# Moving hosted node batches of a four-layer GNN kernel between passes: a quarter of the last node pair goes from the third score pass to the fourth dense slot pass

## The chip, the cores and the metric

One core of one Trainium2 chip runs the whole kernel as a single launch. The metric is the device time of one execution in microseconds (us). Time before: 5043.83 us, the median of three runs (5041.87, 5043.83 and 5056.84 us).

## The reference, cut to what matters

The network is a residual chain over 50,000 nodes and 25,000 edges (sorted by destination), all in float32 with 128 features:

```
x = LN(x + GAT3(x))        # three attention layers, 4 heads, softmax over incoming edges
x = LN(x + GCN2(x))        # two weighted graph convolutions, relu after each
x = LN(x + relu(GCN1(x)))  # one graph convolution
x = LN(x + SAGE2(x))       # relu([h, mean of neighbours] @ W + b), twice
```

Only nodes that are the destination of an edge need the sums over edges. For a node without incoming edges a layer is a dense product with its own row alone: for the SAGE stage `h1 = relu(h W1[0:128] + b1)`, `h2 = relu(h1 W2[0:128] + b2)`, `out = LN(h + h2)`. The intermediate `h1` is needed too, since edges gather it in the second SAGE layer.

## The kernel before, in words

**Tiles.** A batch is 512 rows (four groups `g` of 128), 256 KB. There are `nb` = 49 batches of edge slots and 2 x 49 = 98 batches of nodes. Each table in DRAM (`tables[0]` to `tables[7]`, `final`) has a slot part and a node part. Slot rows carry the destinations with edges, node rows carry every node as if it had none, and the last pass scatters the slot results over the node rows of the output.

**Stages.** The program runs stages one after the other, each in its own block with a barrier of all engines and a clearing of semaphores between two of them (`Semaphores.__exit__`). In order: structure, weights, a dense chain over the nodes, first slots, then three times `edge_scores`, `softmax` and `attend` (one attention layer each), then five passes of `convolve`: convolve(0) and (1) are the two weighted GCN layers, (2) the third GCN layer, (3) and (4) the two SAGE layers.

**Node work rides on edge stages.** `edge_scores` computes attention scores of the edge batches and beside them, on the otherwise free engine time, the dense pair "W1, relu, W2, relu, residual, layer norm" of node batches. For the third layer this pair is the SAGE pair (`third`), and its 98 node batches are spread over three places:

- `edge_scores(2, ..., 0, middle)` with `middle` = 25: 25 turns of one edge batch and two node batches (node batches 0 to 49), with the step orders `step_two`.
- `edge_scores(2, ..., middle, nb, True)` ("solo"): 24 turns of one edge batch and one node batch (the even ones, 50 to 96), with `step_solo`.
- convolve(0) "hosts" the odd ones from 49 to 97 (25 batches, 49 is computed twice), every second turn.

In the first part of a layer's pass with `start` = 0 the kernel also repairs the last rows of each tile (`patch`): POOL gathers `tails`, SP stores them back, and only then do the gathers and the loads of own rows begin.

**Turns and lags.** Every engine has its own hand-written order of steps. `skewed` calls `step(at)` once per turn n; `at(k)` is batch n - k, so a step with `at(3)` works three turns behind. `even(b)` restricts a hosted step to every second batch. All waits are semaphore waits in that in-order stream. Turns of different engines are tied only by these waits.

**convolve.** Per turn, POOL issues four indirect gathers of 128 rows (line 2540) and holds for b > 3 on `summed` of three batches ago. SP loads the batch's own rows (2488), stores the results (2500). DVE builds the selection matrix from a key (`build`, 2828 and 2832), adds the carry between tiles after PE's sum (`carry`, 1913 to 1920) and does the relu out of PSUM (`residual`, 2844). PE sums the edges (`sum_edges`, 2572), adds the own rows (`add_own`: GCN 2587 as a product with a diagonal into the same bank, SAGE 2582 as transposes into a bank of its own) and multiplies by the weights (`product`: 2596, in SAGE also 2599). ACT sets the bias (2698), and copies the sums out (`sums_out`: 2717, in SAGE first the transposed own rows, 2715); in GCN it also builds the diagonal (2702, 2706).

**Hosted chain of one node batch.** SP `load_nodes` (2470, holds on the read of the batch two hosted batches ago), PE `node_turn` (2608), ACT `node_turned` (2734), PE `node_hidden` (2613), ACT `node_relu` (2739), PE `node_middle` (2618), ACT `node_middle_out` (2745, 2747), PE `node_product` (2624), DVE `node_residual` (2880) and `node_moments` (2886, 2891), ACT `node_deviation` (2753), DVE `node_scale` (2897, 2899), ACT `node_normalise` (2759), and two stores on SP (2476, 2482). It has two `nx` and two `nz` buffers. In DVE's order `node_residual` stands behind `residual` of the same turn:

```
b = at(2)
if b:
    residual(b)
b = at(5)
if even(b):
    node_residual(b)
    node_moments(b)
```

Of the kernel before, what the change touches and what calls it, by code (L numbers as in the profile page):

```python
# [15 lines left out]
D = 128  # L16
# [131 lines left out]
def program(nc, io, n_nodes, n_edges):  # L148
# [5 lines left out]
    with ctx:  # L154
# [2250 lines left out]
        def convolve(n, mode, norm, t_in, t_out, t_res, weights, bias_io, nodes=None):  # L2405
# [4 lines left out]
            with ExitStack() as c, Semaphores(nc) as sem:  # L2410
# [35 lines left out]
                def even(b):  # L2446
                    return nodes and b and b.slot % 2 == 0
# [6 lines left out]
                with nc.Block() as block:  # L2454
                    @block.sync
                    def _(sp):
# [45 lines left out]
                        def step(at):  # L2502
                            b = at(0)
                            if b:
                                load_own(b)
                            b = at(1)
                            if b and norm:
                                load_residual(b)
                            b = at(3)
                            if even(b):  # L2510
                                load_nodes(b)
                            b = at(6 if norm else 4)
                            if b and not placing:
                                store(b)
                            b = at(6)
                            if even(b):
                                store_node_middle(b)
                            b = at(9)
                            if even(b):
                                store_nodes(b)  # L2520
                        skewed(sp, nb, 9 if nodes else 6 if norm else 4, step, 4)
# [34 lines left out]
                    def _(pe):  # L2556
# [71 lines left out]
                        def node_steps(at):  # L2628
                            b = at(4)
                            if even(b):  # L2630
                                node_middle(b)
                            b = at(5)
                            if even(b):
                                node_product(b)
                            b = at(3)
                            if even(b):
                                node_hidden(b)

                        def step_gcn_relu(at):
                            b = at(1)  # L2640
                            if b:
                                sum_edges(b)
                            node_steps(at)
                            b = at(2)
                            if b:
                                product(b)
                            if even(b):
# [38 lines left out]
                        if sage:  # L2686
                            skewed(pe, nb, 5 if nodes else 3 if norm else 2, step_sage_norm if norm else step_sage_relu, 4)
                        else:
                            skewed(pe, nb, 5 if nodes else 2, step_gcn_norm if norm else step_gcn_relu, 4)

                    @block.scalar
                    def _(act):
# [70 lines left out]
                        def node_steps(at):  # L2763
                            b = at(3)
                            if even(b):
                                node_relu(b)
                            b = at(4)
                            if even(b):
                                node_middle_out(b)
                            b = at(6)  # L2770
                            if even(b):
                                node_deviation(b)
                            b = at(7)
                            if even(b):
                                node_normalise(b)

                        def step_relu(at):
# [4 lines left out]
                            b = at(2 if sage else 1)  # L2782
# [3 lines left out]
                            b = at(2)  # L2786
# [31 lines left out]
                        else:  # L2818
                            skewed(act, nb, 7 if nodes else 2 if sage else 1, step_relu, 4)

                    @block.vector
                    def _(dve):
# [79 lines left out]
                        def step_relu(at):  # L2902
# [6 lines left out]
                            b = at(6)  # L2909
# [5 lines left out]
                            b = at(5)  # L2915
# [35 lines left out]
                        else:  # L2951
                            skewed(dve, nb, 6 if nodes else 2, step_relu, 4)
# [31 lines left out]
        convolve(0, "gcn0", False, t[3], t[4], None, (io["L1_gnn_W1"],), io["b_L1_gnn_b1"], third + (2 * (nb - middle) + 1,))  # L2984
        convolve(1, "gcn0", True, t[4], t[5], t[3], (io["L1_gnn_W2"],), io["b_L1_gnn_b2"])
        convolve(2, "gcn1", True, t[5], t[6], t[5], (io["L2_gnn_W"],), io["b_L2_gnn_b"])
        convolve(3, "sage", False, t[6], t[7], None, (io["L3_gnn_W1"][D:, :], io["L3_gnn_W1"][0:D, :]), io["b_L3_gnn_b1"])
# [63 lines left out]
```

How the kernel before makes its waits and increments, by code:

```python
def hold(eng, sem, value):  # L76
    if not isinstance(value, int) or value > 0:
        eng.wait_ge(sem, value)
# [12 lines left out]
    def step(self, ins):  # L92
        self.n += 1
        ins.then_inc(self.sem, 1)
        self.eng.wait_ge(self.sem, self.turn.count(self.per_turn, self.n) if self.turn else self.n)
# [122 lines left out]
        def segments(dve, ch, pe_sem, tr_sem, cnt, what, val):  # L218
# [3 lines left out]
            src, src2 = (keep, keep2) if what == "sum" else (pen, pen2)  # L222
            for d, out in ((0, seg_f), (1, seg_b)):
                rev = slice(None, None, -1) if d else slice(None)
                for h in range(4):
                    ins = nc.vector.tensor_tensor_scan(out[:, h, rev], src[:, d, rev], val[:, h, rev],
                                                       neutral, *ops)
                ch.step(ins)
                edge = 0 if d else ROW - 1
                nc.vector.tensor_copy(seg_t[:, :], out[:, :, edge]).then_inc(pe_sem, 1)
                cnt[0] += 1
                dve.wait_ge(tr_sem, cnt[0])
                ch.step(nc.vector.tensor_tensor_scan(seg_s[:, rev], src2[:, d, rev],
                                                     bank[0][0:4, 0:rq][:, rev], neutral, *ops))
                ch.step(nc.vector.memset(seg_c[:, :], neutral))
# [4 lines left out]
                ins.then_inc(pe_sem, 1)  # L240
                cnt[0] += 1
                dve.wait_ge(tr_sem, cnt[0])
                ch.step(nc.vector.tensor_copy(seg_t[:, :], bank[1][0:rq, 0:4]))
```

## Time and profile before

| what | us |
|---|---|
| median of three runs | 5043.83 |
| the profiled execution, its own time | 5052.05 |
| its span, first to last instruction | 5049.9 |
| third score pass, two-node part, 25 turns | 213.9 |
| third score pass, one-node part, 24 turns | 152.1 |
| convolve(0), which hosts, 49 turns | 272.9 |
| convolve(3), which hosts nothing, 49 turns | 257.5 |
| mean granted clock of TensorE (share of full speed) | 0.913 |

The stage times are distances between the barriers, read from the timeline. All durations further down come from the one profiled execution of 5052.05 us. That is 8.2 us over the median and within the three runs shown.

### The profile page before, as it was taken

What the parts mean: (1) busy time and instruction counts of PE and PEld (TensorE: products, weight loads), DVE (VectorE), ACT (ScalarE), POOL (GpSimd) and SP (SyncE); (2) the same over time, 40 slices, a digit from 0 to 9 for tenths busy, and PEclk for the clock granted to TensorE, in tenths of its full rate; (3) what the DMA queues carried; (4) which work ended last, traced back from release to release, by engine and by line L of the source; (5) the groups of instructions that cost most, each with busy time, mean ns of one, the idle gap of its engine ahead of it and who ended that gap; (6) DMA issues with size and microseconds to landing.
All of it is one profiled execution on the core that took longest, in us unless ns stands there. A gap on an engine that the chain in (4) does not pass through costs nothing. (4 is left out here: it accounts for less than half of the span.)

```text
span 5049.9 us, 108087 instructions
## 1 busy us (share of the span) xinstructions
PE 3969.3 (79%) x24378; PEld 2916.8 (58%) x24378; DVE 3727.1 (74%) x14651; ACT 3450.8 (68%) x11317; POOL 3018.4 (60%) x2914
## 2 busy tenths in 40 slices
PE   1999999797996898994998974997877666666554
PEld 1667667565774454873555752444766565665554
DVE  4899999545998787897886966997668787544433
ACT  0789999554886676894776863887878787333332
POOL 6888888255452122761224462887757676767777
PEclk9999999798998899997998997998998898997666
DMA  2566666487996576994777984775766565543332
GB/s 90 157 186 200 196 195 197 161 308 258 351 349 220 196 240 203 357 362 146 241 242 243 333 305 141 228 227 169 234 202 208 187 210 187 153 145 115 93 101 70
DMA packets 603571, 1061.32 MB, mean 210 GB/s; under 512 B 109737, under 2 KB 124603, under 8 KB 603373
## 3 DMA queue, kind: packets, MB, share of 16 engines
q1 hardware_dynamic: 521644, 920.61, 53.4%
q0 software_dynamic: 81728, 138.51, 10.6%
q8 instruction: 70, 1.15, 0.1%
q14 instruction: 129, 1.05, 0.1%
HBM read 608.75 MB, written 453.92 MB: 210 GB/s over the span
## 5 line engine op out<-in xcount | busy, mean ns | idle before, releaser
L2540 POOL DMA_INDIRECT got_c<-table,src_row x980 | 931.4, 950 | 387.7 <-issue 311.9
L1434 POOL DMA_INDIRECT src_got_s<-table,src_row x588 | 554.6, 943 | 445.9 <-issue 93.0
L2572 PE MATMUL bank<-pick_c,got_c 128*128 128x128 f32 x1960 | 333.3, 323 | 352.9 <-DMA got_c<-table,src_row 281.5
L2082 PE MATMUL bank<-w_all,dt_m 128*128 128x512 f32 x1176 | 569.2, 601 | 35.2 <-DMA dt_m<-delta_t 34.0
L2572 PEld LDWEIGHTS bank<-pick_c,got_c 128*128 128x128 f32 x1960 | 288.1, 226 | 396.5 <-issue 244.6
L2056 POOL TENSOR_TENSOR part_m<-part_m,half_sum_m 128x512 f32<-128x512 f32 x98 | 158.6, 1619 | 581.8 <-DVE half_sum_m L2289 581.8
L1607 ACT ACTIVATE z_s<-z_s,shift_s,dev_s 128x128 f32<-128x128 f32 x1080 | 444.0, 485 | 2.2 <-DVE shift_s L1745 1.3
L793 PEld LDWEIGHTS bank<-w_mean,ht 128*128 128x128 f32 x2352 | 312.1, 193 | 142.5 <-issue 142.5
L2596 PE MATMUL bank<-w_c,agg_c 128*128 128x128 f32 x1960 | 370.5, 315 | 4.0 <-ACT agg_c L2717 3.8
L2717 ACT COPY agg_c<-bank 128x512 f32<-128x512 f32 x245 | 142.8, 583 | 320.3 <-DVE bank L1920 274.5
L790 PE MATMUL bank<-bias,first_row 128*128 128x512 f32 x588 | 321.3, 628 | 38.0 <-ACT ht L853 13.8
L2082 PEld LDWEIGHTS bank<-w_all,dt_m 128*128 128x128 f32 x1176 | 210.2, 193 | 231.1 <-issue 133.7
L2596 PEld LDWEIGHTS bank<-w_c,agg_c 128*128 128x128 f32 x1960 | 325.1, 230 | 19.8 <-issue 11.5
L843 ACT ACTIVATE bank<-bank 128x128 f32<-128x128 f32 x1176 | 306.8, 261 | 42.0 <-PE bank L793 33.9
L2183 ACT ACTIVATE part_m<-bank,now_m 128x128 f32<-128x128 f32 x588 | 215.0, 366 | 157.7 <-PE bank L2082 141.2
L793 PE MATMUL bank<-w_mean,ht 128*128 128x128 f32 x2352 | 313.2, 277 | 0.0
L2728 ACT ACTIVATE z_c<-z_c,shift_c,dev_c 128x128 f32<-128x128 f32 x588 | 242.2, 482 | 89.0 <-DVE shift_c L2868 89.0
L2832 DVE TENSOR_SCALAR pick_c<-iota,now_c 128x128 f32<-128x128 f32 x980 | 282.3, 365 | 11.8 <-DVE now_c L2828 0.5
L754 POOL TENSOR_TENSOR rows<-rows 128x512 f32<-128x512 f32 x196 | 260.5, 1329 | 42.9 <-DVE rows L925 40.7
L2061 POOL DMA_INDIRECT x_m<-in_x_dram,dst_node x196 | 222.0, 1133 | 98.5 <-issue 52.0
L1913 DVE COPY tails_c<-tails_c 128x1 f32<-128x1 f32 x245 | 37.5, 153 | 328.4 <-PE bank L2572 322.5
L2289 DVE SCALAR_TENSOR_TENSOR part_m<-bank,now_m,part_m 128x128 f32<-128x128 f32 x588 | 203.6, 346 | 69.5 <-ACT half_sum_m L2184 68.2
(352 smaller groups left out, 11912.6 us busy)
## 6 DMA issues: line engine op xcount, KB each, us to landing
table<-rows SPq DMA_DIRECT2D x294, 256.0 KB
x_s<-table SPq DMA_DIRECT2D x270, 256.0 KB
x_c<-table SPq DMA_DIRECT2D x245, 256.0 KB
table<-z_s SPq DMA_DIRECT2D x196, 256.0 KB
table<-z_c SPq DMA_DIRECT2D x196, 256.0 KB
table<-mid_s SPq DMA_DIRECT2D x172, 256.0 KB
own_rows_s<-table SPq DMA_DIRECT2D x147, 256.0 KB
pick_t_s<-picks_t SPq DMA_DIRECT2D x147, 256.0 KB
```

The source lines that it names most:

```text
L754: nc.gpsimd.tensor_tensor(flat(rows[l + 1][r]), flat(rows[l + 1][r]), flat(rows[l][r]), ALU.add).then_inc(summed[l], 1)
L790: nc.tensor.matmul(b_y[l][:, :], first_row[:, :], bias[:, l, :, :].rearrange("p g d -> p (g d)"), start=True, stop=False, skip_group_check ...
L793: ins = nc.tensor.matmul(b_y[l][:, g * D:(g + 1) * D], ht[l][b.half][:, g, :], w_mean[:, l, :], start=False, stop=True, skip_group_check=True)
L843: ins = nc.scalar.activation(bank[7][:, g * D:(g + 1) * D], b_y[l][:, g * D:(g + 1) * D], ACT.Square, accum_out=square[l][r][:, g:g + 1])
L1434: nc.gpsimd.indirect_dma_start(out=src_got[r][:, g, :], out_offset=None, in_=tables[l].rows, in_offset=bass.IndirectOffsetOnAxis(ap=src_ro ...
L1607: ins = nc.scalar.activation(v[:, g, :], v[:, g, :], ACT.Identity, bias=shift[side(b, h)][:, g:g + 1], scale=dev[side(b, h)][:, g:g + 1])
L2082: nc.tensor.matmul(b_h[k % n_h][:, :], dt[b.slot][:, k, :], w_all[:, l, :, :].rearrange("p h d -> p (h d)"), start=True, stop=True).then_i ...
L2540: nc.gpsimd.indirect_dma_start(out=got[r][:, g, :], out_offset=None, in_=t_in.rows, in_offset=bass.IndirectOffsetOnAxis(ap=src_row[:, t:t ...
L2572: ins = nc.tensor.matmul(b_sum[r][:, k * P:(k + 1) * P], got[b.slot][:, k, :], pick[r][:, k, :], start=k == 0, stop=sage, skip_group_check ...
L2596: ins = nc.tensor.matmul(b_y[r][:, k * D:(k + 1) * D], agg[r][:, k, :], ws[0][:, :], start=False, stop=True, skip_group_check=True)
L2728: ins = nc.scalar.activation(z[b.slot][:, g, :], z[b.slot][:, g, :], ACT.Identity, bias=shift[r][:, g:g + 1], scale=dev[r][:, g:g + 1])
L2832: ins = nc.vector.tensor_scalar(pick[r][:, k, :], iota[:, :], now[r][:, k, KEY:KEY + 1], now[r][:, k, COEF + m:COEF + m + 1], ALU.is_equal ...
```

## The change

It does four things. The third score pass becomes one part of 49 turns in its one-node form, which covers the even node batches 0 to 96. convolve(0) hosts the same odd batches 49 to 97 as before. convolve(3), the first SAGE pass, hosts the odd batches 1 to 49. In every hosted pass all steps of the hosted chain come two turns sooner (the load three), and the pass has two turns less at its end. In a SAGE pass that hosts, ACT copies the sums out one turn sooner (`at(1)` in place of `at(2)`).

```diff
@@ SP in convolve
-                            b = at(3)
+                            b = at(0)
                             if even(b):
                                 load_nodes(b)
                             b = at(6 if norm else 4)
                             if b and not placing:
                                 store(b)
-                            b = at(6)
+                            b = at(4)
                             if even(b):
                                 store_node_middle(b)
-                            b = at(9)
+                            b = at(7)
                             if even(b):
                                 store_nodes(b)
-                        skewed(sp, nb, 9 if nodes else 6 if norm else 4, step, 4)
+                        skewed(sp, nb, 7 if nodes else 6 if norm else 4, step, 4)
@@ PE in convolve: node_middle at(4) to at(2), node_product at(5) to at(3), node_hidden at(3) to at(1)
                             b = at(2)
                             if b:
                                 product(b)
+                            b = at(0)
                             if even(b):
                                 node_turn(b)
...
-                            skewed(pe, nb, 5 if nodes else 3 if norm else 2, step_sage_norm if norm else step_sage_relu, 4)
+                            skewed(pe, nb, 3 if nodes or norm else 2, step_sage_norm if norm else step_sage_relu, 4)
                         else:
-                            skewed(pe, nb, 5 if nodes else 2, step_gcn_norm if norm else step_gcn_relu, 4)
+                            skewed(pe, nb, 3 if nodes else 2, step_gcn_norm if norm else step_gcn_relu, 4)
@@ ACT in convolve: node_relu at(3) to at(1), node_middle_out at(4) to at(2), node_deviation at(6) to at(4), node_normalise at(7) to at(5)
                             node_steps(at)
-                            b = at(2 if sage else 1)
+                            b = at(2 if sage and not nodes else 1)
                             if b:
                                 set_bias(b)
                                 sums_out(b)
-                            b = at(2)
+                            b = at(0)
                             if even(b):
                                 node_turned(b)
...
-                            skewed(act, nb, 7 if nodes else 2 if sage else 1, step_relu, 4)
+                            skewed(act, nb, 5 if nodes else 2 if sage else 1, step_relu, 4)
@@ DVE in convolve: node_scale at(6) to at(4), node_residual and node_moments at(5) to at(3)
-                            skewed(dve, nb, 6 if nodes else 2, step_relu, 4)
+                            skewed(dve, nb, 4 if nodes else 2, step_relu, 4)
@@ the program
-        middle = (nb + 1) // 2
+        spare = nb // 2 * 2 + 1
         third = (t[6], t[7], t[8], (io["L3_gnn_W1"][0:D, :], io["c_L3_gnn_b1"]), (io["L3_gnn_W2"][0:D, :], io["b_L3_gnn_b2"]))
-        edge_scores(2, third[3], third[4], *third[0:3], 0, middle)
-        edge_scores(2, third[3], third[4], *third[0:3], middle, nb, True)
+        edge_scores(2, third[3], third[4], *third[0:3], 0, nb, True)
         softmax(2)
         attend(2)
-        convolve(0, ..., third + (2 * (nb - middle) + 1,))
+        convolve(0, ..., third + (spare,))
         ...
-        convolve(3, "sage", False, t[6], t[7], None, ..., io["b_L3_gnn_b1"])
+        convolve(3, "sage", False, t[6], t[7], None, ..., io["b_L3_gnn_b1"], third + (1,))
```

## Rows read from the trace of the kernel before

**Rows 1.** The page, part 1: busy us, share of the span, instructions.

```profile
PE 3969.3 (79%) x24378; PEld 2916.8 (58%) x24378; DVE 3727.1 (74%) x14651; ACT 3450.8 (68%) x11317; POOL 3018.4 (60%) x2914
```

**Rows 2.** Windows, four stages: stretch, length, busy PE PEld DVE ACT POOL, clock, DMA, GB/s.

```profile
2704.50:2918.40 213.90, 192.04 (x1404) 150.14 (x1404) 177.29 (x675) 163.88 (x401) 96.39 (x102) 0.94 0.90 311
2918.40:3070.50 152.10, 119.45 (x916) 87.97 (x916) 95.22 (x336) 90.56 (x217) 90.61 (x96) 0.94 0.86 294
3487.30:3760.20 272.90, 221.11 (x1632) 191.41 (x1632) 177.13 (x766) 217.81 (x569) 185.31 (x196) 0.96 0.69 216
4284.40:4541.90 257.50, 173.34 (x1376) 160.91 (x1376) 125.42 (x491) 82.99 (x148) 186.15 (x196) 0.96 0.51 152
```

**Rows 3.** Windows of the steady middle of the one-node and the two-node part.

```profile
2950.00:3040.00 90.00, 78.45 (x635) 58.83 (x634) 65.56 (x231) 62.34 (x150) 66.54 (x71) 1.00 0.99 340
2750.00:2870.00 120.00, 118.32 (x902) 93.02 (x901) 113.83 (x434) 105.25 (x259) 61.33 (x66) 1.00 1.01 353
```

**Rows 4.** Line 1712, once per turn: two-node part, then one-node part.

```profile
L1712 DVE TENSOR_TENSOR delta_s<-src_got_s,bank x25: 653/686/690, 2725.9 to 2905.5; 128x512 f32<-128x512 f32 x25
...
L1712 DVE TENSOR_TENSOR delta_s<-src_got_s,bank x24: 672/673/686, 2931.7 to 3057.2; 128x512 f32<-128x512 f32 x24
```

**Rows 5.** The longest wait of PE in the steady one-node part: total, times, longest.

```profile
PEld bank L1501 <- DVE delta_s L1712: 18.8, 12, 1.6
```

**Rows 6.** The gathers of line 2540 in convolve(0), then in convolve(3).

```profile
L2540 POOL DMA_INDIRECT got_c<-table,src_row x196: 940/944/1048, 3488.3 to 3732.2; - x196
...
L2540 POOL DMA_INDIRECT got_c<-table,src_row x196: 940/944/1061, 4285.8 to 4530.5; - x196
```

**Rows 7.** Line 2880, once per hosted batch, in convolve(0).

```profile
L2880 DVE SCALAR_TENSOR_TENSOR nz_c<-bank,nx_c x25: 678/680/693, 3519.1 to 3752.7; 128x512 f32<-128x512 f32 x25
```

**Rows 8.** Timeline of convolve(0), its last full pair of turns and its end.

```profile
3731.16 0.68 DVE L2880 SCALAR_TENSOR_TENSOR nz_c<-bank,nx_c 128x512 f32<-128x512 f32 x1
3731.93 0.34 SPq L2470 DMA_DIRECT2D nx_c<-table  x1
...
3734.94 0.63 PE L2608 MATMUL bank<-ident,nx_c 128*128 128x128 f32 x4 [0.84 <-ACT nmid_c L2745]
3735.40 1.06 PE L2587 MATMUL bank<-own_c,x_c 128*128 128x128 f32 x8
...
3736.50 1.16 PE L2572 MATMUL bank<-pick_c,got_c 128*128 128x128 f32 x8
3737.50 1.06 PE L2624 MATMUL bank<-nw_c,nht_c 128*128 128x128 f32 x8
...
3738.39 1.02 PE L2613 MATMUL bank<-nxt_c,nw_c 128*128 128x512 f32 x2
3739.25 1.05 PE L2596 MATMUL bank<-w_c,agg_c 128*128 128x128 f32 x8
...
3740.34 0.69 DVE L2844 TENSOR_SCALAR z_c<-bank 128x512 f32<-128x512 f32 x1 [1.95 <-PE bank L2596]
3740.95 0.68 DVE L2880 SCALAR_TENSOR_TENSOR nz_c<-bank,nx_c 128x512 f32<-128x512 f32 x1
...
3742.72 1.16 PE L2596 MATMUL bank<-w_c,agg_c 128*128 128x128 f32 x8 [1.09 <-ACT agg_c L2717]
...
3745.08 0.66 PE L2608 MATMUL bank<-ident,nx_c 128*128 128x128 f32 x4 [1.20 <-DMA nx_c<-table]
...
3755.55 1.65 ACT L2759 ACTIVATE nz_c<-nz_c,nshift_c,ndev_c 128x128 f32<-128x128 f32 x4 [0.44 <-DVE nshift_c L2899]
```

**Rows 9.** Timeline of one turn of convolve(3).

```profile
4401.89 0.58 ACT L2715 COPY own_c<-bank 128x512 f32<-128x512 f32 x1
...
4402.75 1.13 PE L2572 MATMUL bank<-pick_c,got_c 128*128 128x128 f32 x8 [1.82 <-DVE pick_c L2832]
4403.72 0.39 PE L2596 MATMUL bank<-w_c,agg_c 128*128 128x128 f32 x2
...
4405.50 0.60 PE L2582 MATMUL bank<-ident,x_c 128*128 128x128 f32 x4
```

More of the change, by code:

```diff
@@ L2628, in node_steps @@
                         def node_steps(at):
-                            b = at(4)
+                            b = at(2)
                             if even(b):
                                 node_middle(b)
-                            b = at(5)
+                            b = at(3)
                             if even(b):
                                 node_product(b)
-                            b = at(3)
+                            b = at(1)
                             if even(b):
@@ L2763, in node_steps @@
                         def node_steps(at):
-                            b = at(3)
+                            b = at(1)
                             if even(b):
                                 node_relu(b)
+                            b = at(2)
+                            if even(b):
+                                node_middle_out(b)
                             b = at(4)
                             if even(b):
-                                node_middle_out(b)
-                            b = at(6)
-                            if even(b):
                                 node_deviation(b)
-                            b = at(7)
+                            b = at(5)
                             if even(b):
@@ L2785, in step_relu @@
                                 sums_out(b)
-                            b = at(2)
+                            b = at(0)
                             if even(b):
@@ L2908, in step_relu @@
                                 carry_over(b)
-                            b = at(6)
+                            b = at(4)
                             if even(b):
@@ L2914, in step_relu @@
                                 residual(b)
-                            b = at(5)
+                            b = at(3)
                             if even(b):
@@ L2977, in program @@
         attend(1)
-        middle = (nb + 1) // 2
+        spare = nb // 2 * 2 + 1
         third = (t[6], t[7], t[8], (io["L3_gnn_W1"][0:D, :], io["c_L3_gnn_b1"]), (io["L3_gnn_W2"][0:D, :], io["b_L3_gnn_b2"]))
-        edge_scores(2, third[3], third[4], *third[0:3], 0, middle)
-        edge_scores(2, third[3], third[4], *third[0:3], middle, nb, True)
+        edge_scores(2, third[3], third[4], *third[0:3], 0, nb, True)
         softmax(2)
         attend(2)
-        convolve(0, "gcn0", False, t[3], t[4], None, (io["L1_gnn_W1"],), io["b_L1_gnn_b1"], third + (2 * (nb - middle) + 1,))
+        convolve(0, "gcn0", False, t[3], t[4], None, (io["L1_gnn_W1"],), io["b_L1_gnn_b1"], third + (spare,))
         convolve(1, "gcn0", True, t[4], t[5], t[3], (io["L1_gnn_W2"],), io["b_L1_gnn_b2"])
         convolve(2, "gcn1", True, t[5], t[6], t[5], (io["L2_gnn_W"],), io["b_L2_gnn_b"])
-        convolve(3, "sage", False, t[6], t[7], None, (io["L3_gnn_W1"][D:, :], io["L3_gnn_W1"][0:D, :]), io["b_L3_gnn_b1"])
+        convolve(3, "sage", False, t[6], t[7], None, (io["L3_gnn_W1"][D:, :], io["L3_gnn_W1"][0:D, :]), io["b_L3_gnn_b1"], third + (1,))
         convolve(4, "sage", True, t[7], t[8], t[6], (io["L3_gnn_W2"][D:, :], io["L3_gnn_W2"][0:D, :]), io["b_L3_gnn_b2"])
```

## The prediction

> **What bounds the kernel now.** The page comes first: PE is busy 79% of the span, DVE 74%, POOL 60% [rows 1]. No engine is full, so the share says little and each stage has to be read for itself. The stages are serial, with a barrier between two of them. So the time of a change is the sum of what it does to the length of each stage that it touches, and the windows give those: 213.9 us for the two-node part of the third score pass, 152.1 for its one-node part, 272.9 for convolve(0), 257.5 for convolve(3) [rows 2].
>
> In the two-node part PE is the bound: busy 118.3 of 120 us in the steady middle [rows 3]. A turn takes (2905.5 - 2725.9) / 24 = 7.48 us [rows 4]. In the one-node part PE is busy 78.5 of 90 us and POOL 66.5 of 90 [rows 3]; PE waits for DVE's difference and DVE for PE, a chain over engines inside a turn [rows 5]. Its turn takes (3057.2 - 2931.7) / 23 = 5.46 us [rows 4].
>
> The convolve passes are bound by something else. POOL issues 196 gathers in (3732.2 - 3488.3) us in convolve(0) and in (4530.5 - 4285.8) us in convolve(3) [rows 6]. Over 195 intervals that is 1.251 and 1.255 us each, 5.00 and 5.02 us per turn of four. Both passes run at POOL's pace although one hosts node work and the other doesn't. What the hosting costs before is the tail: from the last gather's issue to the barrier convolve(0) takes 3760.2 - 3732.2 = 28.0 us, convolve(3) 4541.9 - 4530.5 = 11.4 us [rows 2, 6].
>
> The reading in a sentence: a node batch costs 7.48 - 5.46 = 2.0 us as second node batch in the score pass, and nearly nothing in a pass that waits for POOL anyway.
>
> **Part 1, the score pass in one part.** Before: 213.9 + 152.1 = 366.0 us [rows 2]. After: 49 one-node turns. The head comes from the two-node part, since that one has the repair of tile tails in front: 2725.9 - 2704.5 = 21.4 us to the first use of line 1712 (the one-node part, without the repair, needs 2931.7 - 2918.4 = 13.3). Then 48 turns of 5.46 = 262.1 us. Then the end of the one-node part, 3070.5 - 3057.2 = 13.3 us [rows 2, 4]. The sum is 296.8, so this part gives **-69.2 us**. A barrier, a head of 13.3 and an end are saved once, and 25 turns shrink by 2.0 us each. Bounds of the turn: not under POOL's 5.0 us [rows 6], which would give 22 us more; not over the two-node turn of 7.48, which does strictly more. I take 5.46, since it is the same code. The SP queue gets per turn the same DMAs that it has now in the one-node part.
>
> **Part 2, hosted steps two turns sooner in convolve(0).** In the body every hosted step keeps its place relative to the others and the parity of its turn, so nothing changes there: POOL still sets 5.0 us. Only SP's load comes three turns sooner in its order and not two. It holds on the read of the `nx` buffer by line 2880, and now that hold stands in front of the stores and the two next loads of own rows. Those are needed two turns later and more, and a load lands in about 3 us (3731.93 to 3734.94, [rows 8]), so I cost it at nothing; if that cover were gone PE would wait for own rows. At the end the last node batch was turned at 3745.08, two turns after 3734.94, and the barrier came at 3760.2 [rows 2, 8]. Now the last batch takes the place that the one before it had, 10.1 us sooner. But its steps then stand between the edge steps of the last real turns instead of in empty ones. Its chain, step by step from rows 8: hidden 3738.4; last edge product after the copy at 3742.7; node product right behind at 3743.8; then what the old last batch needed from its own residual to the barrier. That was 3760.2 - 3752.7 = 7.5 us [rows 2, 7], and the residual comes at about 3744.9, or at 3746 if it has to wait for the store of its `nz` buffer. Barrier at 3752.4 to 3753.5: **-7 us** (bounds 0 and -10).
>
> **Part 3, hosting in convolve(3).** Added per pair of turns: three DMAs of 256 KB on SP, PE's 4 + 4 transposes, hidden and product, five ACT operations and the normalise, DVE's residual, moments and scale. Three questions.
>
> First, the tail. It follows the chain of part 2: last sum, node product, hidden, product, last product, node product, 7.5 us. I expect about 20.5 us where convolve(3) had 11.4: **+9 us**, and 1 us for the second weight product in it.
>
> Second, the ring that closes over two turns: residual of a node batch, load into its buffer, `node_turn`, own rows, sum, node product, hidden, product, `residual`, `node_residual`. In convolve(0) it is, from rows 8: 0.77 + 3.01 + 0.46 + 1.10 + 1.00 + 0.89 + 0.86 + 1.09 + 0.61 = 9.79 us, just under POOL's 10.0 for two turns. The mean over the 22 periods from 3519.1 to 3740.95 is 10.08 [rows 7, 8]. In SAGE the own rows are transposes, about 0.46 like `node_turn`, in place of 1.10: -0.64. The product is twice as many matmuls, 4405.50 - 4403.72 = 1.78 in place of about 0.89 [rows 9]: +0.89. So the ring is 10.04 at its fastest and 10.08 + 0.25 = 10.33 by the mean. It then is as long as POOL's ten or a bit longer, and has nothing left to catch up with. 24 pairs times 0.04 to 0.33 is 1 to 8 us. I take **+7 us**, nearer to the mean, since landings vary.
>
> Third, ACT's copies, which move a turn sooner. In rows 8 a sum's copy ends 4.3 us after hidden starts (3738.39 to the product at 3742.72), and SAGE adds the copy of own rows, 0.58 us by the same kind of copy (convolve(3) does one a turn). PE wants it after hidden 0.86, product 1.78, transposes 0.46, sum 0.97 and middle 0.46, that is 4.5 us [rows 8, 9]. So PE waits about 0.4 us once per pair. But `node_turn` then waits for its load in any case: 0.86 + 1.98 + 0.61 + 0.77 + 3.01 = 7.2 us after hidden, against 4.9 + 1.78 = 6.7. The wait is covered by the ring; without that cover it would cost 24 x 0.4 = 10 us.
>
> What POOL does is not altered. In convolve(0) DVE is busy 177.1 us with the hosted steps, in convolve(3) 125.4, and POOL's gathers come every 1.251 and 1.255 us [rows 2, 6]: hosted DVE work does not slow them. The Trainium skill (SBUF — State Buffer, section SBUF: two separate sides) speaks against this change here: it says that GpSimd and certain DVE operations take turns on a shared port, so that descriptors for gathers can't be written meanwhile. The trace disagrees for these operations, as the 1.251 us shows.
>
> **The sum.** -69 - 7 + 10 + 7 = -59 us. Against the profiled execution's own 5052.05 that is 4993. This execution lies 8.2 us over the median of 5043.83, so I forecast **4985 us**. TensorE's granted clock stays as it is in these windows: 1.00 in the steady parts, 0.94 to 0.96 with heads and tails [rows 2, 3].
>
> **The rivals.**
>
> *POOL's pace holds in convolve(3).* The ring comes out at its fast value of 10.04. For it: convolve(0) holds 5.00 with a ring of 9.79. Against it: nothing is left to catch up a late landing. The +7 becomes about 0: 4977 us.
>
> *The copies bind every turn.* If PE's product waited for ACT each turn as in the last full turn of convolve(0), 1.09 us [rows 8], a pair of turns would cost PE's own work plus 2.2. That work is 2 x (0.46 + 0.97 + 1.78) + 0.46 + 0.86 + 0.46 + 0.89 = 9.1 us, so a pair takes 11.3, and 24 x 1.3 = 31 in place of 7: 5009 us. For it: the margin above is only 0.5 us. Against it: ACT has 83 of 257 us busy there now [rows 2].
>
> *POOL stands still while DVE does hosted work.* Hosted DVE work per turn is about (177.1 - 125.4) / 49 = 1.1 us net of what GCN and SAGE share [rows 2]. If that held POOL, 49 x 1.1 = 52 us would come on top of convolve(3), in place of the 7: 5030 us. The gather intervals speak against it. This is the rule of the Trainium skill named above.
>
> *The long one-node pass is slower than its half: slower than before.* The 16 DMA engines show a share of 0.99 in it already, at 340 GB/s [rows 3]. A pass of 24 turns can live on lead and buffers where one of 49 can't, and the gathers would be late. The price is at most the two-node turn: 48 x (7.48 - 5.46) = 97 us more, 5082 us. It decides from the point where a turn takes 5.46 + 59 / 48 = 6.7 us. Against it: the two-node part moved 353 GB/s steadily [rows 3], and the 23 turns show no growth that would lead there.
>
> *The earlier steps don't shorten the tail.* The last node batch waits for an edge step and the barrier stays: 7 to 10 us lost, 4994 us.
>
> **How the numbers follow.** Forecast 0.60; POOL's pace holds 0.18; tail not shorter 0.05; copies bind 0.11; POOL held by DVE 0.02; long pass slower 0.02; the rest for smaller mishaps near the forecast. The range goes from 4966 (POOL's pace, tails at their good bounds, a median that falls as low as the runs before) to 5008 (just to the copies case). About 0.3% (15 us, the spread of the runs before) is what a measurement of this kernel can tell from no change, so faster means under 5029: 0.95. Same 0.03, slower 0.02.
>
> **What the profile after would show.** Line 1712 49 times in one stage of about 297 us, 5.4 to 5.6 apart; a stage over 310 makes part 1 wrong. Line 2540 in convolve(0) as before, and its barrier about 20 to 21 us after the last gather. In convolve(3) line 2608 100 times with a wait for `nx_c`, line 2880 10.0 to 10.4 apart, gathers 5.0 apart, the stage at 271 to 276 us. A wait of PE's 2596 for ACT's 2717 over 0.5 us in most turns would make the third point wrong; gathers over 1.3 us apart without a hold would bring the port back in.

## The result, and the profile after

The changed kernel takes **4979.83 us** (median of 4 runs, 4972.77 to 4991.71) against 5046.00 for the kernel before on the same chip (4 runs, 5041.87 to 5056.84). The ratio is 0.9868 with a 95% interval of 0.9843 to 0.9893: 66 us or 1.3% faster. The forecast was 4985.

The profiled execution of the changed kernel took 4980.41 us, its span is 4978.6, and the page's part 1 answers to [rows 1] almost unchanged:

```profile
PE 3945.6 (79%) x24376; PEld 2889.4 (58%) x24376; DVE 3694.1 (74%) x14601; ACT 3468.5 (70%) x11366; POOL 3017.6 (61%) x2914
```

The same work is done by the same engines (99 node batches in all before and after, 25 of them moved from the score pass into convolve(3)), so the shares tell nothing of the gain. The stages do. Windows of the changed kernel, from barrier to barrier, in the columns of [rows 2]: the third score pass, convolve(0), convolve(3).

```profile
2696.90:2994.70 297.80, 239.58 (x1866) 177.48 (x1866) 194.13 (x686) 184.39 (x442) 187.00 (x198) 0.96 0.90 306
3412.20:3678.20 266.00, 218.68 (x1632) 191.45 (x1632) 176.65 (x766) 217.56 (x569) 185.70 (x196) 0.97 0.70 222
4201.60:4470.10 268.50, 237.32 (x1828) 210.44 (x1828) 173.76 (x766) 175.55 (x373) 186.12 (x196) 0.97 0.69 220
```

| stage | before | after | measured | forecast |
|---|---|---|---|---|
| third score pass | 213.9 + 152.1 = 366.0 | 297.8 | -68.2 | -69.2 |
| convolve(0) | 272.9 | 266.0 | -6.9 | -7 |
| convolve(3) | 257.5 | 268.5 | +11.0 | +17 |
| sum | 896.4 | 832.3 | -64.1 | -59 |

The profiled executions differ by 5052.05 - 4980.41 = 71.6 us. The 7.5 us beyond the sum lie mostly in stages that the change doesn't touch: the barrier in front of the third score pass comes at 2696.9 instead of 2704.5. Such stages move by several us from one execution to the next, so 64 us is the change's part, and the medians' 66.2 agree.

The two-node part is gone, and the one-node turn is what it was. Line 1712 of the changed kernel, once per turn, beside [rows 4]:

```profile
L1712 DVE TENSOR_TENSOR delta_s<-src_got_s,bank x49: 669/673/686, 2718.6 to 2982.6; 128x512 f32<-128x512 f32 x49
```

(2982.6 - 2718.6) / 48 = 5.50 us per turn over the whole length. The gathers of line 2540 in convolve(0) and convolve(3) of the changed kernel, beside [rows 6], and the residual of the hosted batches in both (line 2882, the line 2880 of [rows 7]):

```profile
L2540 POOL DMA_INDIRECT got_c<-table,src_row x196: 938/944/1056, 3413.3 to 3657.5; - x196
...
L2540 POOL DMA_INDIRECT got_c<-table,src_row x196: 940/944/1054, 4202.7 to 4447.3; - x196
...
L2882 DVE SCALAR_TENSOR_TENSOR nz_c<-bank,nx_c x25: 678/681/693, 3436.0 to 3670.6; 128x512 f32<-128x512 f32 x25
...
L2882 DVE SCALAR_TENSOR_TENSOR nz_c<-bank,nx_c x25: 678/681/692, 4227.2 to 4462.7; 128x512 f32<-128x512 f32 x25
```

The gathers of convolve(3) take 244.6 us from first to last; without hosting they took 4530.5 - 4285.8 = 244.7. That is 1.254 us each against 1.255: the body of the pass didn't get longer at all. All of the +11 is tail: 4470.1 - 4447.3 = 22.8 us from the last gather to the barrier, where it was 11.4. In convolve(0) the tail went from 28.0 to 3678.2 - 3657.5 = 20.7 us.

Timeline of the changed kernel, one pair of turns in convolve(3), the ring that the prediction feared (start, duration, engine, line; in brackets the engine's idle time before it and what ended it):

```profile
4327.34 0.68 DVE L2882 SCALAR_TENSOR_TENSOR nz_c<-bank,nx_c 128x512 f32<-128x512 f32 x1
...
4328.27 0.35 SPq L2470 DMA_DIRECT2D nx_c<-table  x1
...
4328.70 0.30 PEld L2596 LDWEIGHTS bank<-w_c,agg_c 128*128 128x128 f32 x2 [0.27 <-ACT agg_c L2719]
...
4331.01 0.66 PE L2608 MATMUL bank<-ident,nx_c 128*128 128x128 f32 x4 [0.26 <-DMA nx_c<-table]
...
4331.50 0.60 PE L2582 MATMUL bank<-ident,x_c 128*128 128x128 f32 x4
...
4331.94 1.06 PE L2572 MATMUL bank<-pick_c,got_c 128*128 128x128 f32 x8
...
4332.83 1.06 PE L2624 MATMUL bank<-nw_c,nht_c 128*128 128x128 f32 x8
...
4333.73 1.02 PE L2613 MATMUL bank<-nxt_c,nw_c 128*128 128x512 f32 x2
...
4334.59 0.39 PE L2596 MATMUL bank<-w_c,agg_c 128*128 128x128 f32 x2
...
4336.57 0.69 DVE L2846 TENSOR_SCALAR z_c<-bank 128x512 f32<-128x512 f32 x1 [1.81 <-PE bank L2599]
...
4337.18 0.68 DVE L2882 SCALAR_TENSOR_TENSOR nz_c<-bank,nx_c 128x512 f32<-128x512 f32 x1
```

From residual to residual: 0.93 to the load's issue, 2.74 to its landing, then 0.49 + 0.44 + 0.89 + 0.90 + 0.86 + 1.98 + 0.61, in sum 9.84 us, under POOL's 10.03 for two turns (eight gathers at 244.6 / 195 us). PE waits 0.26 us for the load, and its weight load 0.27 us for ACT's copy of the sum.

### The profile page after: what moved, and what is told of

It reads as the page before. It is cut to its first block and busy times, and to the rows that moved or that the text cites. A ratio compares the mean times of both kernels' runs of the same rounds, so it can differ in the third digit from the quotient of the medians.

```text
span 4978.6 us, 108273 instructions
## 1 busy us (share of the span) xinstructions
PE 3945.6 (79%) x24376; PEld 2889.4 (58%) x24376; DVE 3694.1 (74%) x14601; ACT 3468.5 (70%) x11366; POOL 3017.6 (61%) x2914
## 5 line engine op out<-in xcount | busy, mean ns | idle before, releaser
L1607 ACT ACTIVATE z_s<-z_s,shift_s,dev_s 128x128 f32<-128x128 f32 x980 | 403.0, 485 | 2.0 <-DVE shift_s L1745 0.9
```

What stands on the lines that cost most here:

```text
L1607: ins = nc.scalar.activation(v[:, g, :], v[:, g, :], ACT.Identity, bias=shift[side(b, h)][:, g:g + 1], scale=dev[side(b, h)][:, g:g + 1])
```

## The experiments

They ran on three chips, four kernels on each. One, called A here, is like that of the result: the kernel before takes 5044.89 us there (median of 7). On B and C it takes 5604.75 and 5661.18 (one run each): the stages with gathers are longer there, for a cause that stays open (see the last section). So stages are compared within a chip. Three kernels ran on B and again on C, and one on B and again on A. All of these are single runs but `last_batch_once`, which has four. The stage lengths are barrier to barrier, from windows.

**What does hosting cost and save in all?** Nothing is hosted; all node batches sit in a two-node score pass in one part:

```
-        edge_scores(2, third[3], third[4], *third[0:3], 0, nb, True)
+        edge_scores(2, third[3], third[4], *third[0:3], 0, nb)
-        convolve(0, ..., third + (spare,))
+        convolve(0, ...)
-        convolve(3, ..., third + (1,))
+        convolve(3, ...)
```

> All 98 node batches in a two-node third score pass of 49 turns, nothing hosted in convolve(0) and convolve(3); the whole computation is done. My theory (a node batch costs 2.0 us as second one in the score pass and only a tail where it is hosted): score pass 213.9 + 24 x 7.48 = 393 us against 297.8 of the changed kernel; convolve(0) falls from 266.0 to about 258 and convolve(3) from 268.5 to 257.5. In sum some 76 us slower than the changed kernel, about 5056. Rival (hosted work stretches the POOL-paced passes by its engine time): convolve(0) and (3) would fall by more than their tails, to under 250 us, and their gathers would come closer than 1.25 us apart.

On B: 5567.87 us, stages 404.8, 305.5 and 303.8. The expected numbers were those of the result's chip. The same kernel on a chip like it:

> The kernel of all_in_pair_pass once more, for a second chip. As before: score pass 393 us, convolve(0) about 258, convolve(3) 257.5, in sum some 76 us slower than the changed kernel, where POOL's gathers come 1.25 us apart.

On A: 5054.82 us. Windows of the three stages:

```profile
2696.10:3088.80 392.70, 367.22 (x2748) 286.35 (x2748) 347.60 (x1323) 321.30 (x785) 186.93 (x198) 0.98 0.95 330
3506.00:3762.90 256.90, 183.94 (x1180) 169.53 (x1180) 127.82 (x491) 121.68 (x344) 185.41 (x196) 0.85 0.51 152
4286.60:4544.90 258.30, 173.23 (x1376) 160.69 (x1376) 124.75 (x491) 82.94 (x148) 186.25 (x196) 0.96 0.50 151
```

The stages came as expected (393, 258 and 257.5 us). They are three points of one ledger. Nothing hosted: 392.7 + 256.9 + 258.3 = 907.9. One pass hosts (before): 896.4. Two passes host (after): 832.3. A pass that hosts a quarter pays 266.0 - 256.9 = 9.1 us in convolve(0) and 268.5 - 258.3 = 10.2 in convolve(3); with the late steps of before it paid 16.0. The second quarter takes 68.2 us off the score pass, the first only 26.7, because it also split the pass in two. The next kernel measures that:

**How much of the 68 us is the barrier?** The one-node pass in two parts, hosting as in the changed kernel (names of tiles and semaphores of the second part apart):

```
-        edge_scores(2, third[3], third[4], *third[0:3], 0, nb, True)
+        edge_scores(2, third[3], third[4], *third[0:3], 0, middle, True)
+        edge_scores(2, third[3], third[4], *third[0:3], middle, nb, True)
```

> The changed kernel with its one-node score pass cut at 25 edge batches into two stages with a barrier between. My theory (the cut costs a second head of 13.3 and a second end of 13.3 us, less one turn of 5.46 that the two ends share): both parts together 297.8 + 21 = 319 us. So of the 68 us that the third score pass gained about 21 are the barrier and about 47 the cheaper turns. Rival (all of the gain is cheaper turns, the barrier costs its few instructions): under 300 us.

> The kernel of one_node_in_two_parts once more. My theory: both parts together 297.8 + 21 = 319 us, the barrier with its second head and end; the rest as in the changed kernel. Rival (the barrier costs its few instructions): under 300 us.

On B, 5583.21 us; the windows of the two parts:

```profile
2813.00:3017.20 204.20, 133.14 (x954) 97.68 (x954) 100.43 (x350) 93.81 (x226) 96.66 (x102) 0.88 0.71 229
3017.20:3205.80 188.60, 130.84 (x916) 96.57 (x916) 96.03 (x336) 90.25 (x217) 90.75 (x96) 0.89 0.73 237
```

Sum 392.8, where a kernel with one part takes 371.8 on the same chip (the next but one): +21.0. On C, 5667.88 us: 206.6 + 188.4 = 395.0 against 370.1: +24.9. So a second part costs 21 to 25 us on these two chips; it wasn't run on a chip like A, where the expectation of 21 rests on the rows of before. If it costs the same there, what is left of the 68, some 43 to 47 us, is the cheaper turns of 25 batches. That evens out the ledger above: 26.7 + 21 to 25 for the first quarter, 68.2 less as much for the second, 43 to 52 us each. The prediction's own split was a head of 13.3, an end, and 25 turns at 2.0 us.

**Are the sooner steps worth 7 us alone?** The placement of before, two passes and all, with the sooner steps:

```
+        middle = (nb + 1) // 2
-        edge_scores(2, third[3], third[4], *third[0:3], 0, nb, True)
+        edge_scores(2, third[3], third[4], *third[0:3], 0, middle)
+        edge_scores(2, third[3], third[4], *third[0:3], middle, nb, True)
-        convolve(3, ..., third + (1,))
+        convolve(3, ...)
```

> The kernel before with the earlier hosted steps alone; distribution of the node batches as before. My theory: only the end of convolve(0) changes, 272.9 to 266 us, every other stage as before, so 7 us faster than the kernel before. Rival (the last node batch waits for the edge steps anyway): convolve(0) stays within 1 us of 272.9. Rival (the load, now in front of the stores in SP's order, delays them): convolve(0)'s body grows and line 2880 comes more than 10.2 us apart.

> The kernel of steps_sooner_only once more. My theory: convolve(0) 266 us in place of 272.9, two-node part 213.9 and one-node part 152.1 as before, so 7 us faster than the kernel before, some 5038. Rival (the last node batch waits anyway): convolve(0) within 1 us of 272.9.

On B 5607.01 us against 5604.75 of the kernel before, on C 5648.38 against 5661.18. One run each, differences of both signs, and no profile of the kernel before on these chips whose convolve(0) could be set beside theirs (328.6 and 332.0). This is inconclusive: no run shows the sooner steps alone on a chip like A. The -7 rests on convolve(0) before and after, 272.9 to 266.0, where the step order is all that differs; the after side came again as 266.0 in `last_batch_once`, the before side is one execution.

**What is the copy a turn sooner worth?** ACT copies the sums at the old place in the hosting pass too:

```
-                            b = at(2 if sage and not nodes else 1)
+                            b = at(2 if sage else 1)
```

> The changed kernel, but ACT copies the sums of the hosting SAGE pass at(2) again. My theory: PE's product of a turn then waits for a copy that ACT makes in the same turn behind its hosted steps: about 4 us in the turns with relu and normalise (0.69 + 1.65 + 0.58 + 0.58 + 0.58 after hidden), about 3 us in the others, so a pair of turns takes about 16 us in place of 10 and convolve(3) about 268 + 24 x 6 = 412 us. Rival (buffers and slack cover it, the move is worth nothing): convolve(3) stays within 5 us of 268.5.

> The kernel of sums_at_two once more. There a pair of turns took 19.8 us, (5136.9 - 4662.2) / 24, against my 16, with PE waiting 3.0 to 3.8 us per turn for ACT's copy and its product of 16 matmuls taking 3.4 us in place of 1.8 behind the wait. Theory A (that chip was slow in all): 16 us a pair here, convolve(3) about 412 us. Theory B (the waits let TensorE's granted clock fall, so the wait costs twice): 19 to 20 us a pair here too, convolve(3) about 505 to 515, and a granted clock well under 1 in its windows.

On B 5778.98 us, convolve(3) 527.7 where the sooner copy takes 331.8 there; on C 5812.70 us, 528.1 against 334.7. That is far more than expected. The windows on B of the whole stage and of four us inside a turn, then rows of the product in two turns that follow each other:

```profile
4616.80:5144.50 527.70, 338.05 (x1828) 308.38 (x1828) 173.64 (x766) 175.57 (x373) 185.52 (x196) 0.75 0.36 112
4816.00:4820.00 4.00, 3.90 (x18) 3.90 (x19) 0.08 (x1) 0.04 (x1) 0.00 (x0) 0.50 0.06 16
```

```profile
4816.10 0.80 PE L2596 MATMUL bank<-w_c,agg_c 128*128 128x128 f32 x2 [3.78 <-ACT agg_c L2719]
...
4819.67 1.06 PE L2582 MATMUL bank<-ident,x_c 128*128 128x128 f32 x4
...
4825.64 0.80 PE L2596 MATMUL bank<-w_c,agg_c 128*128 128x128 f32 x2 [2.87 <-issue]
```

The copy stands behind ACT's hosted steps in the very turn that needs it. PE idles 3.78 us for it in one turn and 2.87 in the next, and then works at a granted clock of 0.50, which is 1.2 of 2.4 GHz: from the start of the product of 16 matmuls to the next step it takes 4819.67 - 4816.10 = 3.57 us instead of 1.78 [rows 9]. The mean clock of the stage is 0.75. The changed kernel has 0.93 over its convolve(3) on C, so it is not the chip. The wait costs twice: itself, and slower matmuls after it. The Trainium skill (TensorE: Matmul & The Clock Gate, section The HAM clock gate) says that PE gets its full or half its clock by how busy it has been; the 0.50 behind an idle 3.78 us agrees. A pair of turns takes (5136.9 - 4662.2) / 24 = 19.8 us in the mean with the short last one, by line 2882:

```profile
L2882 DVE SCALAR_TENSOR_TENSOR nz_c<-bank,nx_c x25: 678/680/692, 4662.2 to 5136.9; 128x512 f32<-128x512 f32 x25
```

It wasn't run on a chip like A, so the price there is open. But POOL waits in this pass for PE's sums, 228.5 us on B and 228.7 on C, so the pace of the gathers doesn't set its length, and an estimate for A is the same 528 us, some 260 over the 268.5 of the changed kernel. What it shows is that the sooner copy is not a detail but a condition for hosting in this pass at all.

**Is POOL or the ring the bound in convolve(3)?** Two kernels bend the ring, one each way. In the first, the load of a node batch waits for the end of DVE's moments and not only of its residual:

```
-                            hold(sp, nz_read, b.ring(1, -2))
+                            hold(sp, nz_stat, b.ring(1, -2))
```

> The changed kernel; SP's load of a hosted batch waits for the moments of the batch before the last and not only for its residual, which lengthens the ring of two turns by 1.4 us (2882 to the end of 2893 is 2.1 us, the residual alone 0.7). My theory (a ring of 9.8 to 10.0 us stands right below POOL's 10.0): a pair of turns takes 11.2 to 11.4 us in both hosting passes, so convolve(0) and convolve(3) grow by about 24 x 1.25 = 30 us each. Rival (POOL alone sets the pace and the ring has room): both within 3 us of 266.0 and 268.5, or of what the same chip shows for the changed kernel.

On A: 5065.68 us. Windows of convolve(0) and convolve(3), and line 2882 in convolve(3):

```profile
3412.20:3721.00 308.80, 231.66 (x1632) 206.43 (x1632) 176.91 (x766) 217.39 (x569) 185.62 (x196) 0.91 0.60 191
4245.50:4555.70 310.20, 245.65 (x1828) 220.92 (x1828) 177.20 (x766) 176.03 (x373) 185.28 (x196) 0.94 0.60 191
```

```profile
L2882 DVE SCALAR_TENSOR_TENSOR nz_c<-bank,nx_c x25: 679/680/692, 4269.8 to 4548.1; 128x512 f32<-128x512 f32 x25
```

Both stages grow by 42.8 and 41.7 us, where 30 were expected. The mean of the 24 periods in convolve(3) is (4548.1 - 4269.8) / 24 = 11.60 us, but they aren't alike. The last, in the tail, is 4.5 us as in the changed kernel. Of the other 23, 16 lie between 11.1 and 11.5 us (mean 11.32) and 7 between 13.1 and 13.7 (mean 13.25). Windows of a long pair and of one us in it; then rows of the long pair and of a plain one:

```profile
4294.27:4307.47 13.20, 10.98 (x77) 10.07 (x76) 7.19 (x33) 7.06 (x16) 10.14 (x11) 0.87 0.61 196
4301.00:4302.00 1.00, 1.00 (x7) 1.00 (x6) 0.00 (x0) 0.03 (x1) 0.69 (x2) 0.50 1.00 381
```

```profile
4299.66 0.75 PE L2608 MATMUL bank<-ident,nx_c 128*128 128x128 f32 x4 [1.99 <-DMA nx_c<-table]
...
4301.06 1.92 PE L2572 MATMUL bank<-pick_c,got_c 128*128 128x128 f32 x8
...
4407.71 0.68 DVE L2882 SCALAR_TENSOR_TENSOR nz_c<-bank,nx_c 128x512 f32<-128x512 f32 x1
...
4410.10 0.35 SPq L2470 DMA_DIRECT2D nx_c<-table  x1
```

In the plain pair the issue comes 2.39 us after the residual's start instead of 0.93, +1.46. Taken from 11.32 that leaves 9.86 for the ring as it was, beside the 9.84 read directly. The ring of the changed kernel thus stands some 0.2 us under POOL's 10.03. In the long pairs TensorE pays twice, as in `sums_at_two`: it waited 1.88 to 2.53 us for the load, its granted clock fell to 0.50 behind that (0.87 or 0.88 over each of these pairs), and the sum of 8 matmuls took 1.92 us instead of 1.06. In the plain pairs it waited 1.55 to 1.87 us and kept 1.00. So of the growth some 23 x (11.32 - 10.03) = 30 us are the longer ring, as expected, and 7 x (13.25 - 11.32) = 14 the clock.

In the second, DVE does the residual of the hosted batch ahead of that of the edges, which lets the load start sooner:

```
+                            b = at(3)
+                            if even(b):
+                                node_residual(b)
                             b = at(2)
                             if b:
                                 residual(b)
                             b = at(3)
                             if even(b):
-                                node_residual(b)
                                 node_moments(b)
```

> The changed kernel; in DVE's order node_residual stands in front of residual of the same turn, so the ring no longer contains PE's hidden product, the edge product and that residual: some 3 us shorter. My theory (POOL's 10.0 us already held in the changed kernel): the waits of line 2608 for nx_c vanish, 26 us in convolve(3) and 42 in convolve(0), and the stages get at most 2 us shorter. Rival (the ring costs the body something): convolve(3) gets 5 us or more shorter.

On A: 4983.23 us, convolve(0) 267.1, convolve(3) 268.6, within 1.1 and 0.1 us of the changed kernel. What PE waits for ahead of line 2608 in convolve(3), first in the changed kernel, then in this one (us, times):

```profile
L2608 PE MATMUL bank<-ident,nx_c x100: 272/273/418, 4213.7 to 4452.4; 128*128 128x128 f32 x100
...
  DMA nx_c<-table: 25.7, 45
```

```profile
L2608 PE MATMUL bank<-ident,nx_c x100: 272/273/421, 4216.4 to 4454.4; 128*128 128x128 f32 x100
...
  issue: 1.1, 2
```

All 25.7 us of waiting for the load vanish and the stage doesn't move by more than 0.1 us. (In convolve(0) the wait for the load falls from 41.6 to 1.0 us too, but PE stands 44.2 us for other things ahead of the same line.) The ring isn't the bound; POOL is, and PE's wait for the load was time that it had anyway. POOL's own waits for PE's sum in convolve(3) say the same (us in total, times, longest), first in the changed kernel, then in `load_waits_longer`:

```profile
POOL got_c L2540 <- PE bank L2572: 7.3, 24, 0.3
...
POOL got_c L2540 <- PE bank L2572: 37.5, 23, 3.4
```

The sum that POOL holds on is that of four batches before, whose buffer it fills again. In the changed kernel it never stands longer for it than 0.3 us, and that is what it idles ahead of any gather.

**What is the extra batch worth?** With an odd number of batches, batch 49 is computed by convolve(0) and once more by convolve(3). Here convolve(3) leaves it out:

```
-                    n_own = (nb + 1) // 2
+                    n_own = (nb + 1) // 2 - (offset == 1)
...
-                    return nodes and b and b.slot % 2 == 0
+                    return nodes and b and b.slot % 2 == 0 and not (
+                        offset == 1 and isinstance(b.i, int) and b.batch() == nb - 1)
```

> The changed kernel, but convolve(3) leaves out its 25th hosted batch (node batch 49), which convolve(0) computes as well; nothing of the result is missing. My theory: convolve(3)'s tail is the chain of the last node batch; now the batch before it ends it, so the barrier comes 4 to 8 us sooner, 268.5 to about 263 us, and no other stage changes. Rival (the last edge batch holds the end): under 1 us.

On A: 4978.68 us (median of 4 runs, 4972.18 to 4986.30) against 5044.89, ratio 0.987, interval 0.9851 to 0.9888. Window of convolve(3):

```profile
4204.70:4466.80 262.10, 234.01 (x1810) 208.09 (x1810) 170.79 (x755) 171.43 (x364) 185.76 (x196) 0.97 0.70 223
```

262.1 against 268.5: 6.4 us of the 11 were the tail of a batch that need not be there. The other stages are unchanged. In the whole time 6 us are less than the runs resolve (its ratio and that of the changed kernel overlap), so this is the best version by its stage, not shown by its total.

**Does the gain hold on a slower chip?** The changed kernel itself on C:

> The changed kernel itself, as the reference for the others of this call on the same chip. Where POOL's gathers come 1.25 us apart: score pass 297.8, convolve(0) 266.0, convolve(3) 268.5 us, all within 1 us.

5626.20 us against 5661.18 of the kernel before, one run each: -35 us, 0.6%. Line 1712 in the score pass, and the windows of the score pass and convolve(3):

```profile
L1712 DVE TENSOR_TENSOR delta_s<-src_got_s,bank x49: 670/674/689, 2858.6 to 3195.6; 128x512 f32<-128x512 f32 x49
```

```profile
2837.60:3207.70 370.10, 258.17 (x1866) 191.58 (x1866) 197.47 (x686) 183.58 (x442) 187.40 (x198) 0.91 0.77 246
4637.50:4972.20 334.70, 251.08 (x1828) 221.71 (x1828) 176.63 (x766) 175.95 (x373) 186.39 (x196) 0.93 0.58 177
```

A one-node turn takes (3195.6 - 2858.6) / 48 = 7.02 us there. The two-node part of `steps_sooner_only_2` on the same chip:

```profile
L1712 DVE TENSOR_TENSOR delta_s<-src_got_s,bank x25: 652/686/689, 2868.5 to 3061.7; 128x512 f32<-128x512 f32 x25
```

That is (3061.7 - 2868.5) / 24 = 8.05 us, so a second node batch costs 1.0 us there, not 2.0. In the score pass the change gains 227.9 + 189.2 - 370.1 = 47.0 us, of which 24.9 are the barrier. Hosting in convolve(3) costs 334.7 - 307.4 = 27.3 us, not 11. So the cheaper turns (22 us) don't pay for the hosting, and what remains is about the barrier. Whether the kernel that hosts nothing is the better one there stays open. By stages on B it takes 404.8 + 305.5 + 303.8 = 1014.1 us, and the changed placement 371.8 + 328.1 + 331.8 = 1031.7, put together from two kernels. But by whole times it takes 5567.87 us, and `one_node_in_two_parts` less its 21.0 for the second part 5562. The changed kernel itself didn't run on B.

## Why the prediction was right, step by step

**Part 1, the score pass: right.** Forecast 21.4 + 262.1 + 13.3 = 296.8; measured 2718.6 - 2696.9 = 21.7, then 264.0, then 2994.7 - 2982.6 = 12.1, in sum 297.8. The turn is 5.50 for 5.46 over twice the length: lead and buffers of the short pass were not what kept it fast. The rival "the long one-node pass is slower" fell on this chip. On C the turn is 7.02 us, over the 6.7 from which it was to decide, but not by that rival's mechanism: the DMA engines show a share of 0.77 there instead of 0.90, and the one-node part of 24 turns in `steps_sooner_only_2` is as slow (189.2 us for 152.1). What bounds the one-node turn of 5.50 us, the chain between PE and DVE or the DMA engines with their share of 0.99 [rows 3], no run separates.

**Part 2, convolve(0): right.** Forecast -7 with a barrier 20 to 21 us after the last gather; measured -6.9 and 20.7. That the load three turns sooner costs nothing held. The wait ahead of PE's last product for ACT's copy is still 1.09 us, as in [rows 8], and the chain from the last residual to the barrier is 3678.2 - 3670.6 = 7.6 for 7.5.

**Part 3, tail: right, 1.4 us short.** Forecast +10 with the second weight product; measured +11.4. Timeline of the tail in convolve(3) of the changed kernel:

```profile
4459.52 0.49 PE L2596 MATMUL bank<-w_c,agg_c 128*128 128x128 f32 x2 [1.56 <-ACT agg_c L2719]
...
4462.65 0.69 DVE L2882 SCALAR_TENSOR_TENSOR nz_c<-bank,nx_c 128x512 f32<-128x512 f32 x1 [0.35 <-PE bank L2624]
```

From the last residual to the barrier 4470.1 - 4462.65 = 7.45, the forecast's 7.5. The 1.56 us for ACT's copy are 0.5 more than in convolve(0), about one copy of own rows (0.58 us), which ACT does in SAGE only. The rest of the 1.4 us wasn't traced.

**Part 3, ring: the mis-sized term, +7 that measured 0.** The terms of the fast ring were near: 10.04 forecast, 9.84 in the pair shown and 9.86 by `load_waits_longer`. The landing took 2.74 instead of 3.01 us, the issue 0.93 instead of 0.77. What failed is the step "10.08 + 0.25 = 10.33 by the mean". The 10.08 was the period of a pass that POOL paces at 10.00; the ring inside it was shorter and waited. Adding the ring's growth to a period that another chain sets counts slack as cost. The right form is the larger of the two, POOL's 10.03 or the ring, and the body's 244.6 us says that it is POOL's. So the rival "POOL's pace holds in convolve(3)" came out (4977 forecast, 4980 measured). `node_residual_first` shows that shortening the ring gains nothing, `load_waits_longer` that it has some 0.2 us of room to grow. The forecast of the whole came near in spite of this because the term is small beside the 66 us.

**Part 3, copies: right.** Forecast: a wait of about 0.4 us once per pair, covered. In the pair shown it is 0.27 us on the weight load and none on the matmul, and the body is no longer than without hosting. "The copies bind every turn" fell; `sums_at_two` shows what that rival looks like when it is real.

**The rival that POOL stands still: refuted.** With hosted DVE work the gathers come every 1.254 us, without it every 1.255. The Trainium skill (SBUF — State Buffer, section SBUF: two separate sides) says that GpSimd and certain DVE operations lock each other out of a shared port, and names those in a two-port mode or with two inputs in SBUF. The hosted residual has one of its two inputs in PSUM, and the hosted operations as a whole show nothing of a lock here. So this isn't evidence against the rule, and the prediction read it too widely where it set it against this change.

**Range and sum.** The sum was -59 and the stages gave -64.1; the difference is in the main the 7 us of the ring less the small misses of the score pass (1.0) and the tail (1.4). 4979.83 lies inside 4966 to 5008.

## What to carry to other kernels

Look for passes paced by something that isn't computation (here gathers at 1.25 us each): dense work put into them cost its tail, 9 to 11 us per pass, while the same work in a pass bound by TensorE cost 2 us a batch and a barrier with head and end another 21 to 25. Measure it on each chip: on C the hosting cost 27 us. Where a ring of dependences runs beside a pace that another engine sets, take the larger of the two, never their sum, and measure how near they are before leaning on it: here 1.46 us more in the ring cost 42 us per pass. When a copy serves a later matmul, put it ahead of hosted steps on its engine; waits of TensorE of 1.88 to 3.78 us were paid twice in the runs here, the second time as a lower clock.

## What was not expected of the hardware

**Stages with gathers differ from chip to chip.** On B and C every convolve pass measured takes 300 us or more, and the one-node score pass 370. POOL in convolve(3) of the changed kernel on C, and the same gathers there in the kernel without hosting in it (`steps_sooner_only_2`):

```profile
4703.59 1.04 POOL L2540 DMA_INDIRECT got_c<-table,src_row  x1 [1.41 <-DMA table<-nmid_c]
```

```profile
L2540 POOL DMA_INDIRECT got_c<-table,src_row x196: 938/944/990, 4686.3 to 4976.0; - x196
```

The gather itself takes the same 0.94 us, but in the changed kernel the first of a turn's four is mostly preceded by an idle 1.3 to 1.5 us instead of 0.30; without hosting such idle times are fewer, and many of them are 2.3 us. There the mean spacing is (4976.0 - 4686.3) / 195 = 1.49 us against 1.255 on the result's chip. The trace names a store of `nmid_c` as what ended the wait, but `steps_sooner_only_2` issues no such store in this pass, so the releaser is not to be trusted. Nor is it POOL alone. In the score pass of the changed kernel on C four engines stand at the same time:

```profile
3000.13 0.69 DVE L1719 COPY mid_s<-bank 128x512 f32<-128x512 f32 x1 [2.17 <-DMA pick_m<-picks]
3000.28 0.59 ACT L1587 COPY xt_s<-bank 128x512 f32<-128x512 f32 x1 [1.56 <-DMA x_m<-table]
...
3000.51 0.95 POOL L1434 DMA_INDIRECT src_got_s<-table,src_row  x1 [1.35 <-DMA x_m<-table]
...
3000.92 1.12 PE L1457 MATMUL bank<-xt_s,w_s 128*128 128x512 f32 x2 [1.51 <-issue]
```

The tiles named, `pick_m` and `x_m`, belong to another stage. So it isn't shown that the gathers are what is slow on these chips, and the cause stays open.

**A wait of TensorE lowers its clock for the work behind it.** In `sums_at_two` 3.78 and 2.87 us of waiting in two turns brought the granted clock to 0.50 at the next product and to 0.75 over the pass, on two chips alike (527.7 and 528.1 us). In `load_waits_longer` waits of 1.88 to 2.53 us did it in 7 pairs of turns, and waits of 1.55 to 1.87 us in the 16 others left it at 1.00.
